# Deformable convolution: all four corners summed and turned on VectorE, TensorE working by blocks of 6 or 7 tiles

## What is computed

```
x = x + _L3_conv_ref(_gn(x), L3_conv_offset_w, L3_conv_deform_w)
...
p = corner(y0i, x0i, (1 - ly) * (1 - lx))
p = p + corner(y0i, x0i + 1, (1 - ly) * lx)
p = p + corner(y0i + 1, x0i, ly * (1 - lx))
p = p + corner(y0i + 1, x0i + 1, ly * lx)
...
offset = _conv2d(x, offset_w)
patches = _deform_patches(x, offset)
...
y = jnp.einsum('bckhw,ock->bohw', patches, wk)
avg = jnp.mean(y, axis=(2, 3), keepdims=True)
std = jnp.std(y, axis=(2, 3), keepdims=True, ddof=1)
attn = jax.nn.sigmoid(avg + std)
return y * attn
```

## Time and profile before

| what | value |
| --- | --- |
| median of 3 runs | 14692.38 us (14690.25 to 14722.44) |
| the profiled execution, its own time | 14656.86 us |
| its span, first to last instruction | 14654.9 us |
| deform phase, from about | 3728 us to the end |
| mean granted clock of TensorE, whole span | 0.739 of 2.4 GHz |

### The profile page before, as it was taken

The page is one execution under the profiler, slowest core; times in us unless marked ns, Lnnn a source line. Parts: engine busy times, 40 slices in busy tenths (PEclk is TensorE's granted clock), DMA queues, the critical chain, the costliest instruction groups (busy, mean ns, idle before and its releaser), DMA issues.

```text
span 14654.9 us, 154001 instructions
## 1 busy us (share of the span) xinstructions
PE 8240.4 (56%) x51639; PEld 5651.9 (39%) x51639; DVE 6540.2 (45%) x13232; ACT 2973.2 (20%) x5102; POOL 7483.2 (51%) x7657
## 2 busy tenths in 40 slices
PE   6887888889453535444454535354444545353533
PEld 2333444449343433333333434343333333343433
DVE  5655555553235343434344353434343443534343
ACT  3433444433111111111111111111111111111111
POOL 0011222222366666666566666666666666666665
PEclk9998899999676767666676767666666767676766
DMA  3322111117333333333333333333333333333332
GB/s 91 88 81 71 53 57 53 61 47 228 100 97 110 99 107 102 113 94 113 98 107 110 97 108 97 109 103 112 94 113 95 113 109 98 109 97 106 103 96 83
DMA packets 503966, 1436.58 MB, mean 98 GB/s; under 512 B 128981, under 2 KB 234197, under 8 KB 474577
## 3 DMA queue, kind: packets, MB, share of 16 engines
q0 software_dynamic: 353344, 970.88, 22.5%
q1 hardware_dynamic: 150032, 458.00, 10.4%
HBM read 1175.46 MB, written 252.90 MB: 97 GB/s over the span
## 4 chain that ended last, share of the span: by engine, by line
another core or an unknown queue 38%; PE 16%; issue 12%; DVE 3%; ACT 3%; POOL 2%; DMA 0%; ACTq 0%; DVEq 0%; POOLq 0%; SPq 0%
PE e_ps L1939 9%; PE e_ps L1930 3%; POOL e_g L1783 2%; ACT e_corners L1846 2%; PE e_ps L1878 1%; PE e_ps L1889 1%; PE e_ps L1904 1%; DVE e_sty L2099 1%; DVE e_g L2090 1%; DVE e_g L2092 1%; DVE e_big L2112 0%; DVE e_x3t L1964 0%; DMA e_g<-table_dram,e_index_slots 0%; ACT e_pad L1820 0%
## 5 line engine op out<-in xcount | busy, mean ns | idle before, releaser
L1783 POOL DMA_INDIRECT e_g<-table_dram,e_index_slots x7056 | 6787.9, 962 | 4077.6 <-issue 2012.1
L1939 PE MATMUL e_ps<-e_corners,e_w_def 128*64 128x128 f32 x14112 | 2585.5, 358 | 4504.9 <-ACT e_corners L1846 3118.6
L1939 PEld LDWEIGHTS e_ps<-e_corners,e_w_def 128*64 128x64 f32 x14112 | 2280.0, 187 | 4790.6 <-ACT e_corners L1846 3282.8
L1930 PE MATMUL e_ps<-k_ident,e_g 128*128 128x128 f32 x7056 | 1281.1, 327 | 1263.0 <-DVE e_g L2092 654.7
L1846 ACT ACTIVATE e_corners<-e_ps 128x512 f32<-128x512 f32 (+1 forms) x2352 | 1027.0, 489 | 3253.4 <-remote 2383.7
L2060 DVE COPY e_index_slots<-e_index_now 128x9 uint32<-128x9 uint32 x784 | 141.3, 181 | 3272.9 <-DMA e_g<-table_dram,e_index_slots 3222.1
L1930 PEld LDWEIGHTS e_ps<-k_ident,e_g 128*128 128x128 f32 x7056 | 969.2, 168 | 1585.1 <-issue 899.5
L2089 DVE TENSOR_TENSOR e_ps<-e_g,e_ps 128x512 f32<-128x512 f32 (+1 forms) x2352 | 1327.0, 564 | 120.9 <-DMA e_g<-table_dram,e_index_slots 58.5
L1852 ACT ACTIVATE e_big<-e_ps 64x128 f32<-64x128 f32 x784 | 212.6, 271 | 5706.3 <-remote 4282.0
L2092 DVE TENSOR_TENSOR e_g<-e_g,e_ps 128x512 f32<-128x512 f32 (+1 forms) x2352 | 1301.1, 553 | 110.7 <-remote 12.2
L2090 DVE TENSOR_TENSOR e_g<-e_g,e_ps 128x512 f32<-128x512 f32 (+1 forms) x2352 | 1283.6, 546 | 0.0
(11 more groups left out here) (438 smaller groups left out, 8421.3 us busy)
## 6 DMA issues: line engine op xcount, KB each, us to landing
e_g<-table_dram,e_index_slots POOLq DMA_INDIRECT x7056
table_dram<-e_rt SPq DMA_DIRECT2D x32, 1624.0 KB
a_xt<-x_in SPq DMA_DIRECT2D x16, 1568.0 KB
v_dram<-a_vout SPq DMA_DIRECT2D x32, 784.0 KB, 8.5
b_xt<-v_dram SPq DMA_DIRECT2D x16, 1568.0 KB
v_dram<-b_vout SPq DMA_DIRECT2D x32, 784.0 KB, 7.7
c_v2t<-v_dram SPq DMA_DIRECT2D x16, 1568.0 KB
c_xt<-x_in SPq DMA_DIRECT2D x16, 1568.0 KB, 6.5
```

Of the source, the lines that this page charges most:

```text
L1783: pool.indirect_dma_start(out=g[:, slot, tap * CORNERS:(tap + 1) * CORNERS], out_offset=None, in_=table, in_offset=bass.IndirectOffsetOnAx ...
L1930: mm = pe.transpose(ps[:, TURN[tap // 4], (tap % 4) * P:(tap % 4 + 1) * P], g[:, slot, tap * CORNERS:tap * CORNERS + 2 * C], k.ident[:, :])
L1939: mm = pe.matmul(ps[0:C, OUT, 0:P], w_d[:, tap, :], corners[:, tap, :], start=(tap == 0), stop=(tap == TAPS - 1))
```

## The change

DVE now sums all four corners of a tile and turns the sums itself, in 32x32 blocks, into the new buffer `turned`; PE's transposes and ACT's copies of them are gone. A tile takes one multiply of the left side of all 9 taps (L2121), and for each of three batches of 3 taps a multiply (L2127), three adds (L2129, L2130, L2132) and a block transpose from PSUM to `turned` (L2135). POOL's slots are released by DVE's `added`, no more by PE.

PE multiplies by blocks of 6 or 7 tiles (`block_products`, L1924): 18 steps (9 taps, two halves of 32 channels) on each of four groups of 32 partitions, each into its own PSUM bank, 72 matmuls of 192 or 224 columns. There are 8 blocks a pair; `turned` has two halves, so DVE at the first tile of a block waits until the block before the last one is multiplied (`out_done`). ACT copies a block out in 4 instructions (6 where it holds the border between the images). PE's and ACT's share in preparing the next pair moves between blocks 1 to 4, with 6 PSUM banks in rotation instead of 2.

The finish of a pair moves to tiles 4, 5 and 6 of the next one, on 128 partitions instead of twice on 64: 7 statistics instructions, one scale-and-add. The preparation that DVE had at tiles 1 to 8 is now at tiles 8 to 15; positions stay at 34 to 41. SP loads and stores whole pairs. Constants that the deform phase doesn't use are given up before it, to make room.

The core of the diff:

```
--- before.py
+++ after.py
-    ROWS_AT, OFFSETS_AT, TURN_AT, POSITIONS_AT = 9, 16, 30, 34
-    ROW_TURNS, TURN_TILES = H // 4, 13
+    BATCHES = tuple((lo, lo + 3) for lo in range(0, TAPS, 3))
+    BOUNDS = (0, 7, 13, 19, 25, 31, 37, 43, PX_TILES)
+    BLOCKS = tuple(zip(BOUNDS, BOUNDS[1:]))
+    LONGEST, MIDDLE = 7, PX_TILES // 2
+    QUARTER = P // 4
+    ROW_TURNS = H // ROWS
+    FINISH_AT, X3_AT, X3_SUM_AT, STATS_AT, MOMENTS_AT, SCALE_AT, POSITIONS_AT = 4, 8, 10, 11, 13, 15, 34
+    MEANS_BLOCK, ROWS_BLOCK, OFFSETS_BLOCK, TURN_BLOCK = 1, 2, 3, 4
...
-                        pool.wait_ge(bank_done, (r - 1) * (3 * SLOTS) + (3 * slot + 3))
+                        pool.wait_ge(added, (r - 1) * (3 * SLOTS) + (3 * slot + 3))
...
+                def block_out(p, n):
+                    lo, hi = BLOCKS[n]
+                    act.wait_ge(out_done, p * len(BLOCKS) + (n + 1))
...
-                def between(n, at_tile):
-                    if at_tile == MEANS_AT:
-                        pe.wait_ge(st_s, n * 2 + 2)
...
-                    elif ROWS_AT <= at_tile < ROWS_AT + ROW_TURNS // 2:
...
-                    elif OFFSETS_AT <= at_tile < OFFSETS_AT + 2 * N and (at_tile - OFFSETS_AT) % 2 == 0:
...
-                def turn(p, at_tile, between):
...
-                    pe.wait_ge(corners_ready, t * 3)
-                    for tap in range(TAPS):
-                        if tap % 4 == 0:
-                            pe.wait_ge(added, t * 3 + (tap // 4 + 1))
-                        mm = pe.transpose(ps[:, TURN[tap // 4], (tap % 4) * P:(tap % 4 + 1) * P],
...
-                        if tap % 4 == 3 or tap == TAPS - 1:
-                            mm.then_inc(bank_done, 1)
-                    for tap in range(TAPS):
-                        if tap % 4 == 0:
-                            pe.wait_ge(corners_ready, t * 3 + (tap // 4 + 1))
-                        if tap == 0:
-                            pe.wait_ge(out_ready, t)
-                        mm = pe.matmul(ps[0:C, OUT, 0:P], w_d[:, tap, :], corners[:, tap, :],
-                                       start=(tap == 0), stop=(tap == TAPS - 1))
+                def block_products(p, n):
+                    lo, hi = BLOCKS[n]
+                    pe.wait_ge(summed, p * (3 * PX_TILES) + 3 * hi)
+                    need(pe, out_ready, p * len(BLOCKS) + n)
+                    for step_ in range(TAPS * 2):
+                        for q in range(4):
+                            rows = slice(q * QUARTER, (q + 1) * QUARTER)
+                            mm = pe.matmul(ps[:, OUT[q], 0:wide], w_d[rows, step_, :], turned[rows, n % 2, step_, 0:wide],
+                                           start=(step_ == 0), stop=(step_ == TAPS * 2 - 1))
                     mm.then_inc(out_done, 1)
...
+                def pair(p, ahead):
+                    for n in range(len(BLOCKS)):
+                        if ahead is not None:
+                            if n == MEANS_BLOCK:
+                                means(ahead)
+                            elif n == ROWS_BLOCK:
+                                pe.wait_ge(out_ready, p * len(BLOCKS) + n)
+                                columns(ahead)
+                            elif n == OFFSETS_BLOCK:
+                                pe.wait_ge(out_ready, p * len(BLOCKS) + n)
+                                offsets(ahead)
+                            elif n == TURN_BLOCK:
+                                turn_offsets(ahead)
+                            if n == ROWS_BLOCK:
+                                pe.wait_ge(rt_ready, ahead * ROW_TURNS + ROW_TURNS)
+                            elif n == OFFSETS_BLOCK:
+                                pe.wait_ge(off_ready, ahead * N + N)
+                        block_products(p, n)
...
+                def finish(p, part):
+                    c = Chain(dve, final_v, p, 3)
+                    if part == 0:
+                        dve.wait_ge(out_ready, p * len(BLOCKS) + len(BLOCKS))
...
+                    else:
+                        dve.wait_ge(final_a, p * 2 + 2)
+                        dve.wait_ge(x3_back, p * 16 + 16)
+                        dve.scalar_tensor_tensor(big[:, :], big[:, :], fin[:, 4:5], x3t[:, :],
+                                                 ALU.mult, ALU.add).then_inc(x3_used, 1)
...
-                def turn(p, at_tile, between):
+                    if at_tile == lo:
+
+                        need(dve, out_done, p * len(BLOCKS) + (block - 1))
...
-                    for n, (lo, hi) in enumerate(BATCHES):
...
-                        dve.tensor_tensor(half, sides[:, lo:hi, 1, :, :], spread(1), ALU.mult).then_inc(weighted, 1)
-                        dve.tensor_tensor(left, left, spread(0), ALU.mult).then_inc(weighted, 1)
-                        dve.wait_ge(weighted, t * 6 + (2 * n + 2))
-                        dve.tensor_tensor(left, left, half, ALU.add).then_inc(added, 1)
...
-                def finish(p):
-                    dve.wait_ge(out_ready, p * PX_TILES + PX_TILES)
...
+                    left = sides[:, :, 0, :, :]
+                    dve.tensor_tensor(left, left, spread(0, TAPS, 0), ALU.mult).then_inc(weighted, 1)
+                    for n, (a, b) in enumerate(BATCHES):
...
+                        need(dve, summed, t * 3 + n)
+                        dve.tensor_tensor(half, sides[:, a:b, 1, :, :], spread(a, b, 1), ALU.mult).then_inc(weighted, 1)
+                        dve.wait_ge(weighted, t * 4 + (n + 2))
+                        dve.tensor_tensor(upper, upper, half[:, :, 0, :], ALU.add).then_inc(joined, 1)
+                        dve.tensor_tensor(half[:, :, 1, :], lower, half[:, :, 1, :], ALU.add).then_inc(joined, 1)
+                        dve.wait_ge(joined, t * 6 + (2 * n + 2))
+                        dve.tensor_tensor(half[:, :, 0, :], upper, half[:, :, 1, :], ALU.add).then_inc(added, 1)
+                        dve.wait_ge(added, t * 3 + (n + 1))
+                        to = turned[:, block % 2, 2 * a:2 * b, (at_tile - lo) * QUARTER:(at_tile - lo + 1) * QUARTER]
+                        dve.transpose(to.rearrange("p (k h) x -> p k h x", h=2),
+                                      half[:, :, 0, :].rearrange("p k (h x) -> p k h x", x=QUARTER)).then_inc(summed, 1)
...
+                def pair(p, behind, ahead):
+                    for at_tile in range(PX_TILES):
+                        turn(p, at_tile, ahead is None)
+                        if behind is not None and FINISH_AT <= at_tile < FINISH_AT + 3:
+                            finish(behind, at_tile - FINISH_AT)
+                        if ahead is not None:
+                            between(ahead, at_tile)
+                    if ahead is not None:
+                        switch(ahead)
```

319 lines of the change are left out of this document (155 added, 164 removed).

## The result

The changed kernel takes 14971.08 us (median of 4 runs, 14930.75 to 15007.91) against 14704.29 us of the kernel before on the same chip: ratio **1.018**, 95% interval 1.0142 to 1.0218, slower by 1.8%. The forecast was 13,090 us. Its profiled execution has a span of 15005.9 us; the first gather starts at 3850.50 us, the last at 14927.67.

The account below looks back on a forecast made before the run. POOL's gather issue was taken as the bound: 551.6 + 7.5 + 2.1 + 10 = 571, kept as 570.2 us a pair, times 16 = 9123; with start 3871, end 62 and run offsets, 13,090 us; range 12,800 to 14,000.

Parts of the forecast that it names:

- POOL's floor: POOL's gather issue with nothing holding it: 1.251 us a gather, 551.6 us a pair, 11.26 us a tile.
- POOL's release: POOL's slots freed by DVE's `added`, no PE step in a tile's loop: 122.5 us a pair of held time go.
- The prediction's last sentence: Prediction fails if PE's late signals grow further once POOL never pauses; no size or chance given.
- DVE per tile: DVE's work on one new tile: 7.6 us, under POOL's 11.26 us, so it costs nothing.
- Rival C: DVE becomes the bound through dear transposes; at 1.8 us each 625 us a pair, 13,970 us; chance 0.04.
- PE per block: PE's 144 passes for a block of products: 7, 17 or 24 us, taken as 17 us.
- PE's late word: PE's signal reaching other engines late while POOL gathers: 12.5 us, or 45 in an unbroken run.
- A: Late signals from PE stop POOL once a pair, 40 us a pair, 13,730 us; chance 0.20.
- E: No gain: POOL's idle time stays and only changes its name, 14,690 us; chance 0.01.
- B: TensorE becomes the bound if row groups exclude each other: block 83 us, about 17,300 us; chance 0.03.
- D: DVE's transposes hold POOL off, each delaying a gather by 0.25 us: 37 us a pair, 13,680 us; chance 0.04.
- Preparation, finish: Next pair's preparation just covered, 10 us a pair left over; finish's scale-and-add slows one gather by 2.1 us.

## Why the prediction was wrong

- **POOL's floor** (1.251 us a gather, 551.6 us a pair): right; 0.968 + 0.289 = 1.257.
- **The step that failed** is *POOL's release*: "The 122.5 us go if DVE keeps up and nothing else stops it." I had read the earlier trace rows as a signal of PE that reaches others late, a price for each hand-over. It was more than that: PE's own passes come late while POOL gathers without a rest, and so does every step of DVE behind a wait, even for its own semaphores. The 122.5 us did not go, they became 140. From that reading I took the hand-overs out of the loop and expected POOL to run free; but a POOL that runs free is what slows the rest. The prediction's last sentence named this (a lateness that grows once POOL never pauses) without giving it a rival of its own.
- **What the trace of before could have told**: PE's transposes stood singly there too, with nothing to wait for (timelines of PE and DVE):

```profile
6195.40 0.27 PE L1930 MATMUL e_ps<-k_ident,e_g 128*128 128x128 f32 x1 [1.43 <-issue]
6196.77 0.29 DVE L2092 TENSOR_TENSOR e_g<-e_g,e_ps 128x128 f32<-128x128 f32 x1
6198.19 0.37 PE L1930 MATMUL e_ps<-k_ident,e_g 128*128 128x128 f32 x1 [2.52 <-issue]
```

  DVE was not slowed in that kernel: L2092 waits for a semaphore of DVE and stood still for 98.8 us in 2042 times, 0.05 us. The new one has 12 such waits a tile instead of 6 and longer runs of gathers (POOL stopped for more than 2.5 us 14 times a pair, formerly 24 times); which of the two slows DVE was not separated. One more reading was off: "both go on within 3.4 us" after POOL stopped holds for the second copy alone, the first began at 6220.61, 5.2 us before the stop.
- **DVE per tile**, 7.6 us: 7.40 where it runs free, the transpose 0.38 as taken. But 12 steps behind a wait instead of 6 have to be got through, and slowed a tile took about 19 us. Rival C's mechanism in another guise: DVE holds POOL, not because of the transposes' price.
- **PE per block**, 17 us: 6.13 us free at the full clock, 0.043 us a pass, and 13 us (estimate above) at the clock of 0.50. Row groups do overlap: 0.043 lies even below the 0.048 us of my lower bound. Slowed, the block took 56.5 us, and "6 tiles or 68 us later, so 17 us plus PE's late word fits" fell with it: DVE waited 68 us a pair for blocks. The Trainium skill, "TensorE: Matmul & The Clock Gate", section "Why this matters for your kernels", has four row groups side by side; the free block agrees. Bunching the products may have made it worse: the 27 passes of a tile before are fewer than PE sends without a gap after a stop (62 in the block above), the 144 of a block are more. No run tests this.
- **The prediction's rivals.** **A** had a late word once a pair, 40 us; it was 140 us a pair, in some 24 waits. **E**, "POOL's idle time stays and only changes its name", given 0.01, is what came nearest: 140 for 122.5 us. It was set aside by the earlier trace rows, which show POOL's own pace, not what the other engines do at that pace. **B** (no overlap) falls by the free block, **D** by the mean gather of 968 ns, 963 before in the same stretch.
- **Preparation, finish:** their chain never became the bound. DVE stood 12 us a pair for the turned offsets, near the 10 that I had left for it. The start came 17 us earlier instead of 4 later, the tail grew by 25 us instead of 10.

What is shown: while POOL gathers without a break, PE's instructions come late, and so do DVE's steps behind a wait. PE's columns, TensorE's code fetches and the gathers' bytes have no part in it. Rests of POOL free DVE, lessen PE's delay and end POOL's waits, and the rest needed grows with TensorE's passes. What stays open is which part of the chip is short, whether DVE's steps wait for instructions or for semaphores, what makes ACT's copies 10 us late in the earlier trace rows, why single instructions come in steps of about 0.7 us, and whether the profiler's recording takes part; this wasn't tried. Nor was a kernel with fewer VectorE instructions or fewer waits.

## What to carry to other kernels

An idle time without a visible cause ("issue", or "remote" for a step that should be prompt) must be priced per instruction or per wait, and its trigger looked for on the other engines, before a change counts on its going away. Where GpSimd issues small gathers back to back, count the instructions and waits of all other engines and try a short rest for it: 2.2 us after nine gathers gained 4% here on the changed kernel and 1.2% on the one before. A wait that looks like pure loss may be what lets the others run; whoever removes it should time both a version without it and one with a deliberate rest.
